# Leaving out the filler products of four linear-attention layers in an eight-block kernel on one core

## The chip, the cores and the metric

The kernel runs on one core of one Trainium2 chip. The metric is device time in microseconds (us), lower is better. Three runs of the kernel before gave 787.8, 789.82 and 791.66 us; their median is 789.82 us.

## The reference

The input is two images of 32 x 32 positions and 64 channels (2048 tokens). Six blocks follow one another, each adding to its input: a four-way selective scan with a 3x3 convolution and gates, a recurrent complex convolution in 16 steps, a softmax attention over the tokens, a two-of-eight expert layer, a stack of four linear-attention layers with eight heads each, and a spectral filter bank of 16 filters. The change lies in the fifth block. Its core, with Z of shape (2, 1024, 64):

```python
for i in range(n_layer):            # 4
    Zi = Z
    residues = jnp.zeros_like(Zi)
    for j in range(n_head):         # 8
        Attn = jnp.einsum('bni,ij,bmj->bnm', Zi, Q[i, j], Zi)
        values = jnp.einsum('ij,bnj->bni', V[i, j], Zi)
        residues = residues + jnp.einsum('bnm,bmi->bni', Attn, values) / n
    Z = Zi + residues / n_head
```

There is no softmax in it. So all of a layer can be told by the 64 x 64 matrix G = Z^T Z of each image: with S the sum over the heads of Q G V^T, the layer is Z (I + S / (n n_head)), and the next layer's G follows from this one's by two small products.

## The kernel before, in words

Every engine has its own program, written out by hand, and semaphores order them; there is no scheduler. PE works its program strictly in the order in which the code issues it.

The six blocks are stages that follow one another. In the fifth, the normed tokens are held token-major (xn); eight products of 128 x 128 add up G of both images in PSUM bank 2, and xn is turned to xn_t. Then a loop over the four layers works on 128 x 128 matrices alone, each holding the two images as diagonal blocks. Names and lines of one pass:

- L1718 (PE): T = G V for all heads, one product of 256 columns for each row pair and image. It waits for g_ready_0 (from DVE) and g_ready_1 (from ACT).
- L1053 (ACT): copies T from PSUM to t_sb.
- L1725 (PE): four products that add up S over the head pairs.
- L1343 (DVE): is_sb = I + S / (n n_head), one block for each image.
- L1731 (PE): G times is_sb, and L1348 (DVE) copies it to u_sb. L1733 (PE): the product W of all layers so far, and L1055 (ACT) copies it to wt_sb.
- L1736 (PE): the next layer's G, and L488 and L489 copy its blocks to g_two and g_sb, on DVE for the first image, on ACT for the second.

The last layer has neither L1731 nor L1736. In layer 0, ACT also scales four weight matrices (L1059) after L1055. Behind the loop L1739 turns W (ACT's L1064 copies it), L1743 applies it to all tokens, DVE adds the result (L1360), norms the tokens, and PE turns them (L1623) ahead of the filter loop (L1765, L1781).

At three places of a pass stands a call of keep_busy (line 1383; its product is line 1386): a product of the identity with the first 256 columns of the constants into PSUM bank 0, which nobody reads. It waits for nothing and signals nothing. Other such calls stand at lines 1396, 1606, 1632, 1686, 1707 and 1746, ahead of other stages.

Of the kernel before, what the change touches and what calls it, by code (L numbers as in the profile page):

```python
# [67 lines left out]
def wait(engine, sem, value):  # L68

    if isinstance(value, int) and value <= 0:  # L70
        return
    engine.wait_ge(sem, value)

def program(nc, x_cm, consts, vec, rows, w_in, conv_w, w_dt, w_bc, par, w_out, w_gate, ab, dft,
            w_qv, w_k, w_attn, w_router, w_expert, b_expert, v_t, q_t, phi, sigma, m_phi, m_u, out):
    with ExitStack() as ctx:
# [5 lines left out]
        def sig(name):  # L83
            if name not in sems:
                sems[name] = ctx.enter_context(nc.semaphore(name))
            return sems[name]
# [1291 lines left out]
        def _(pe):  # L1378
# [4 lines left out]
            def keep_busy(bank, times, cols=HALF):  # L1383

                for _ in range(times):
                    pe.matmul(ps[:, bank, 0:cols], ident, cst[:, 0:cols], start=True, stop=True)  # L1386
# [328 lines left out]
            for l in range(LAYERS):  # L1715
                for b in range(B):
                    pe.wait_ge(sig(f"g_ready_{b}"), l + 1)
                    mm = pe.matmul(ps[:, 3, b * 256:(b + 1) * 256], g_two[:, b, :], v_sb[:, l, :],  # L1718
                                   start=True, stop=True)
                mm.then_inc(sig("t_done"), 1)  # L1720
                keep_busy(0, 1, 256)
                pe.wait_ge(sig("t_out"), l + 1)
                t_pairs = t_sb.rearrange("p (b h e) -> p b h e", b=B, h=4)
                for h in range(4):
                    mm = pe.matmul(ps[:, 4, 0:P].rearrange("p (b e) -> p b e", b=B), q_sb[:, l, h, :],  # L1725
                                   t_pairs[:, :, h, :], start=(h == 0), stop=(h == 3))
                mm.then_inc(sig("s_done"), 1)
                keep_busy(0, 1, 256)
                pe.wait_ge(sig("is_ready"), l + 1)
                if l < LAYERS - 1:  # L1730
                    pe.matmul(ps[:, 5, 0:P], g_sb, is_sb, start=True, stop=True).then_inc(sig("gs_done"), 1)  # L1731
                wait(pe, sig("wt_out"), l)
                pe.matmul(ps[:, 6, 0:P], is_sb, wt_sb if l else ident, start=True, stop=True).then_inc(sig("wt_done"), 1)  # L1733
                if l < LAYERS - 1:
                    pe.wait_ge(sig("gs_out"), l + 1)
                    pe.matmul(ps[:, 7, 0:P], is_sb, u_sb, start=True, stop=True).then_inc(sig("g_done"), 1)  # L1736
                    keep_busy(0, 1, 256)
            pe.wait_ge(sig("wt_out"), LAYERS)
            pe.transpose(ps[:, 6, 0:P], wt_sb, ident).then_inc(reach("w_turned"), 1)  # L1739
            pe.wait_ge(*after("w_out_ready"))  # L1740
# [207 lines left out]
```

## Time and profile before

| what | value |
|---|---|
| median of three runs | 789.82 us |
| the profiled execution, its own time | 790.21 us |
| its span, first to last instruction | 788.4 us |
| mean granted clock of TensorE over the span | 0.977 |
| PE busy | 713.4 us (90%), 2480 instructions |
| DVE busy | 605.7 us (77%) |
| POOL busy | 413.4 us (52%) |
| ACT busy | 349.9 us (44%) |
| the four layers | 597.2 to 621.3 us of the span |
| fillers (L1386) in the whole program | 110 records, 45.0 us |

Busy time says how long an engine worked, not what waited for it; that is told by the idle time before an instruction and by its releaser, in brackets in the timeline. A product of 32-bit numbers shows as two records in the trace.

### The profile page before, as it was taken

Reading aid. Unit: us, or ns where it says so; the run is one execution under the profiler, and the core shown is the slowest. Engines: PE = TensorE matmul, PEld = TensorE weight load, DVE = VectorE, ACT = ScalarE, POOL = GpSimd, SP = SyncE. Lnnn points to the kernel's source line nnn. Section 1 sums busy time; section 2 is a strip of 40 time slices with the busy share of each in tenths; the row PEclk is TensorE's granted clock in tenths of the full one; section 3 lists DMA queues with packets and bytes.
Section 4 is the critical chain, followed back from the end, with each engine's and each line's share of the span. In section 5 each row is a group of like instructions: output and inputs, shape, how many; then the busy total and the mean of one; then the engine's idle time right before and its main releaser. Section 6 shows DMA issues by size and latency. Waiting matters only on the chain.

```text
span 788.4 us, 7109 instructions
## 1 busy us (share of the span) xinstructions
PE 713.4 (90%) x2480; PEld 358.9 (46%) x2480; DVE 605.7 (77%) x598; ACT 349.9 (44%) x387; POOL 413.4 (52%) x229
## 2 busy tenths in 40 slices
PE   6979999989899899998988868997798899999997
PEld 4633333333233233333333323465345577777775
DVE  5799999999999999999999948656793543334432
ACT  3676474556754754556544326143103243333331
POOL 3166999998999999899889900000051000000000
PEclk9979999999999999999999989999999999999999
DMA  5134564665554646536465451300730000000000
GB/s 169 62 133 140 185 212 168 220 214 175 187 180 166 236 162 207 197 137 202 157 246 176 159 214 81 106 10 1 281 145 1 1 0 1 1 1 0 0 0 27
DMA packets 30126, 97.76 MB, mean 124 GB/s; under 512 B 4132, under 2 KB 4870, under 8 KB 29358
## 3 DMA queue, kind: packets, MB, share of 16 engines
q1 hardware_dynamic: 30096, 97.38, 35.6%
q8 instruction: 16, 0.26, 0.1%
q14 instruction: 14, 0.11, 0.0%
HBM read 95.78 MB, written 1.59 MB: 123 GB/s over the span
## 4 chain that ended last, share of the span: by engine, by line
PE 42%; DVE 28%; issue 11%; POOL 9%; DMA 5%; ACT 4%; SPq 0%; DVEq 0%; POOLq 0%
PE ps L1765 15%; DVE area L1173 10%; PE ps L1460 6%; POOL area L617 6%; DVE ps L1161 5%; DMA area<-c_rows 4%; PE ps L1483 4%; PE ps L1781 4%; DVE area L1169 2%; DVE area L354 2%; PE ps L1386 2%; PE ps L1404 1%; DVE small L432 1%; POOL area L633 1%; PE ps L1451 1%
## 5 line engine op out<-in xcount | busy, mean ns | idle before, releaser
L617 POOL TENSOR_TENSOR area<-area 128x1024 f32<-128x1024 f32 x127 | 297.7, 2370 | 32.0 <-DVE area L1173 21.4
L1483 PE MATMUL ps<-area,cst 128*128 128x512 f32 x512 | 254.2, 623 | 7.1 <-POOL area L617 6.6
L1173 DVE TENSOR_TENSOR_SCAN area<-area,ps 128x1024 f32<-128x1024 f32 x111 | 249.8, 2275 | 4.1 <-ACT area L809 0.9
L809 ACT ACTIVATE area<-area,floors,par_sb 128x1024 f32<-128x1024 f32 x111 | 133.0, 1235 | 62.2 <-DVE area L1173 55.6
L1483 PEld LDWEIGHTS ps<-area,cst 128*128 128x128 f32 x512 | 89.8, 192 | 119.9 <-issue 95.5
L1161 DVE TENSOR_TENSOR ps<-ps,area 128x1024 f32<-128x1024 f32 x111 | 133.0, 1213 | 4.5 <-PE ps L1451 3.9
L1765 PE MATMUL ps<-stack,sel 128*128 128x512 f32 (+1 forms) x576 | 116.2, 362 | 0.7 <-DVE sel L1366 0.7
L1765 PEld LDWEIGHTS ps<-stack,sel 128*128 128x128 f32 x576 | 97.0, 191 | 19.7 <-issue 1.2
L464 DVE COPY area<-ps 64x1024 f32<-64x1024 f32 x32 | 39.3, 1227 | 73.6 <-PE ps L1781 41.4
L714 POOL COPY area<-area 128x256 f32 (+1 forms) x16 | 6.4, 403 | 131.3 <-PE ps L1781 131.3
L462 ACT ACTIVATE area<-ps 64x1024 f32<-64x1024 f32 x32 | 32.7, 1021 | 95.7 <-PE ps L1765 52.8
L1451 PE MATMUL ps<-stack,sel 32*128 32x512 f32 x222 | 54.1, 498 | 18.0 <-DVE area L1173 17.8
L695 POOL TENSOR_TENSOR area<-area 128x256 f32<-128x256 f32 x8 | 5.8, 728 | 120.5 <-DVE area L1319 120.5
L1451 PEld LDWEIGHTS ps<-stack,sel 32*128 32x128 f32 x222 | 20.3, 186 | 95.8 <-DVE area L1173 53.0
L1460 PE MATMUL ps<-area,cst 128*128 128x512 f32 x112 | 50.2, 600 | 6.3 <-DVE area L1173 6.3
L809 ACT ACTIVATE ps<-area,floors,par_sb 128x1024 f32<-128x1024 f32 x17 | 20.5, 1208 | 79.2 <-DVE area L1173 79.2
L1386 PE MATMUL ps<-cst 128*128 128x512 f32 (+1 forms) x110 | 45.0, 551 | 0.0
L633 POOL TENSOR_TENSOR area<-area 128x1024 f32<-128x1024 f32 x17 | 40.0, 2355 | 0.0
L1169 DVE TENSOR_TENSOR_SCAN area<-ps,area 128x1024 f32<-128x1024 f32 x17 | 38.5, 2267 | 0.0
L1460 PEld LDWEIGHTS ps<-area,cst 128*128 128x128 f32 x112 | 20.6, 190 | 34.8 <-issue 23.2
L1354 DVE TENSOR_TENSOR stack<-area,stack 128x1025 fp32r<-128x1025 f32 x16 | 19.5, 1227 | 14.8 <-ACT stack L1070 14.8
L1386 PEld LDWEIGHTS ps<-cst 128*128 128x128 f32 x110 | 21.9, 207 | 17.7 <-issue 16.5
(310 smaller groups left out, 713.2 us busy)
## 6 DMA issues: line engine op xcount, KB each, us to landing
area<-c_rows SPq DMA_DIRECT2D x145, 512.0 KB, 4.4
area<-phi_scaled SPq DMA_DIRECT2D x1, 4104.0 KB, 24.2
area<-in_m_phi_dram SPq DMA_DIRECT2D x4, 1024.0 KB, 8.2
area<-phi_scaled SPq DMA_DIRECT2D x1, 4096.0 KB, 13.8
area<-in_q_t_dram SPq DMA_DIRECT2D x1, 1024.0 KB, 13.7
c_rows<-tok SPq DMA_DIRECT2D x28, 32.0 KB, 2.8
area<-in_dft_dram SPq DMA_DIRECT2D x1, 784.0 KB
area<-in_m_u_dram SPq DMA_DIRECT2D x1, 768.0 KB, 5.8
```

What stands on the lines that cost most here:

```text
L464: engine.tensor_copy(dst, src).then_inc(sig("filtered_1"), 1)
L617: pool.tensor_tensor(scan_order(prod[:, u % PRODS, :], k), lines(state[:, u % STATES, :], k), lines(c_sb[:, u % COPIES, :], k), MUL).then_ ...
L633: pool.tensor_tensor(aid, aid, u_in[:, n % 2, :], MUL).then_inc(sig("pool_driven"), 1)
L809: act.activation(dst, delta[:, n % 2, :], ACT.Exp, bias=floors[:, k, i:i + 1], scale=par_sb[:, k, i:i + 1]).then_inc(sig("decayed"), 1)
L1161: dve.tensor_tensor(drive_pair(u), drive_pair(u), u_in[:, n % 2, :], MUL).then_inc(sig("driven"), 1)
L1169: dve.tensor_tensor_scan(state[:, u % STATES, :], banks(BANK["a", u]), aid, 0.0, MUL, ADD).then_inc(sig("scanned"), 1)
L1173: dve.tensor_tensor_scan(state[:, u % STATES, :], decay[:, u % DECAYS, :], drive_pair(u), 0.0, MUL, ADD).then_inc(sig("scanned"), 1)
L1386: pe.matmul(ps[:, bank, 0:cols], ident, cst[:, 0:cols], start=True, stop=True)
L1451: mm = pe.matmul(ps[:, BANK["b", u] + h, :], sel[at:at + 32, i, :], b_rows[at:at + 32, n % 2, :], start=True, stop=True)
L1460: mm = pe.matmul(ps[:, BANK["soft", n] + h, :], ident, half(term, h), start=(at == 0), stop=(at == 3))
L1483: mm = pe.matmul(ps[:, 6 + h, :], con("center"), half(prod[:, u % PRODS, :], h), start=(u % (UNITS // 2) == 0), stop=(u % (UNITS // 2) == ...
L1765: mm = pe.matmul(ps[:, 2 + 2 * (g % 2) + y, :].rearrange("p (a n) -> p a n", a=2)[:, :, P * (at - 2 * y):2 * P], xn_hl[:, x_part, j * P:(j ...
```

## The change

The three calls of keep_busy inside the layer loop are taken out. Nothing else differs; the other six calls stay.

```diff
@@ -1718,14 +1718,12 @@
                     mm = pe.matmul(ps[:, 3, b * 256:(b + 1) * 256], g_two[:, b, :], v_sb[:, l, :],
                                    start=True, stop=True)
                 mm.then_inc(sig("t_done"), 1)
-                keep_busy(0, 1, 256)
                 pe.wait_ge(sig("t_out"), l + 1)
                 t_pairs = t_sb.rearrange("p (b h e) -> p b h e", b=B, h=4)
                 for h in range(4):
                     mm = pe.matmul(ps[:, 4, 0:P].rearrange("p (b e) -> p b e", b=B), q_sb[:, l, h, :],
                                    t_pairs[:, :, h, :], start=(h == 0), stop=(h == 3))
                 mm.then_inc(sig("s_done"), 1)
-                keep_busy(0, 1, 256)
                 pe.wait_ge(sig("is_ready"), l + 1)
                 if l < LAYERS - 1:
                     pe.matmul(ps[:, 5, 0:P], g_sb, is_sb, start=True, stop=True).then_inc(sig("gs_done"), 1)
@@ -1734,7 +1732,6 @@
                 if l < LAYERS - 1:
                     pe.wait_ge(sig("gs_out"), l + 1)
                     pe.matmul(ps[:, 7, 0:P], is_sb, u_sb, start=True, stop=True).then_inc(sig("g_done"), 1)
-                    keep_busy(0, 1, 256)
             pe.wait_ge(sig("wt_out"), LAYERS)
             pe.transpose(ps[:, 6, 0:P], wt_sb, ident).then_inc(reach("w_turned"), 1)
             pe.wait_ge(*after("w_out_ready"))
```

PE's program of one layer (l=1) before, to the first product of the next; L1386 is the filler, the other names are those of the list above:

```order
L1718 MATMUL ps<-area 128x256 x2
L1386 MATMUL ps<-cst 128x256
L1725 MATMUL ps<-area 128x128 x4
L1386 MATMUL ps<-cst 128x256
L1731 MATMUL ps<-area 128x128
L1733 MATMUL ps<-area 128x128
L1736 MATMUL ps<-area 128x128
L1386 MATMUL ps<-cst 128x256
L1718 MATMUL ps<-area 128x256 x2
```

The same in the changed program, where L1725 has become line 1724, L1731 1729, L1733 1731 and L1736 1734:

```order
L1718 MATMUL ps<-area 128x256 x2
L1724 MATMUL ps<-area 128x128 x4
L1729 MATMUL ps<-area 128x128
L1731 MATMUL ps<-area 128x128
L1734 MATMUL ps<-area 128x128
L1718 MATMUL ps<-area 128x256 x2
```

Three products are gone, and no other has changed its place. In the last layer, with what follows it, PE's program before:

```order
L1718 MATMUL ps<-area 128x256 x2
L1386 MATMUL ps<-cst 128x256
L1725 MATMUL ps<-area 128x128 x4
L1386 MATMUL ps<-cst 128x256
L1733 MATMUL ps<-area 128x128
L1739 MATMUL ps<-cst,area 128x128
L1743 MATMUL ps<-area 128x128 x8
L1386 MATMUL ps<-cst 128x512 x7
```

And in the changed program:

```order
L1718 MATMUL ps<-area 128x256 x2
L1724 MATMUL ps<-area 128x128 x4
L1731 MATMUL ps<-area 128x128
L1736 MATMUL ps<-cst,area 128x128
L1740 MATMUL ps<-area 128x128 x8
L1386 MATMUL ps<-cst 128x512 x7
```

Here two are gone, and the seven fillers behind L1743 stay. In all PE's program is shorter by 11 products; the programs of DVE, ACT and SP are the same, and so is POOL's but for line numbers.

## Rows read from the trace of the kernel before

**Rows 1.** Timeline, one layer (l=2): start, duration, engine, line, xcount [idle before <-releaser].

```profile
610.56 1.13 PE L1718 MATMUL ps<-area 128*128 128x256 f32 x4 [0.33 <-DVE area L489]
...
611.53 0.59 PE L1386 MATMUL ps<-cst 128*128 128x256 f32 x2
611.73 0.60 ACT L1053 ACTIVATE area<-ps 128x512 f32<-128x512 f32 x1 [1.33 <-PE ps L1718]
...
612.38 1.16 PE L1725 MATMUL ps<-area 128*128 128x128 f32 x8 [0.26 <-ACT area L1053]
...
613.38 0.60 PE L1386 MATMUL ps<-cst 128*128 128x256 f32 x2
613.58 0.46 DVE L1343 SCALAR_TENSOR_TENSOR area<-ps,cst 64x64 f32<-64x64 f32 x2 [3.07 <-PE ps L1725]
...
614.09 0.49 PE L1731 MATMUL ps<-area 128*128 128x128 f32 x2
...
614.96 0.49 PE L1736 MATMUL ps<-area 128*128 128x128 f32 x2 [0.16 <-DVE area L1348]
...
615.28 0.60 PE L1386 MATMUL ps<-cst 128*128 128x256 f32 x2
...
615.95 0.22 DVE L489 COPY area<-ps 64x64 f32<-64x64 f32 x1
...
616.22 1.13 PE L1718 MATMUL ps<-area 128*128 128x256 f32 x4 [0.34 <-DVE area L489]
```

**Rows 2.** Groups of PE, 597.2 to 621.3: xcount | busy us, mean ns | idle before.

```profile
L1386 PE MATMUL ps<-cst 128*128 128x256 f32 x22 | 6.6, 380 | 0.0
```

**Rows 3.** Stretch of the layers: length, busy of PE, PEld, DVE, ACT, POOL, then PEclk.

```profile
597.20:621.30 24.10, 18.88 (x93) 12.40 (x92) 4.61 (x20) 8.78 (x28) 3.49 (x4) 1.00 0.00 1
```

**Rows 4.** Timeline between layers 0 and 1, PE and ACT.

```profile
602.53 0.49 PE L1736 MATMUL ps<-area 128*128 128x128 f32 x2 [0.16 <-DVE area L1348]
602.58 2.12 ACT L1059 ACTIVATE area<-area,small 128x384 f32<-128x384 f32 x4
...
603.78 0.70 PE L1718 MATMUL ps<-area 128*128 128x256 f32 x2 [0.34 <-DVE area L489]
...
605.34 0.70 PE L1718 MATMUL ps<-area 128*128 128x256 f32 x2 [0.86 <-ACT area L489]
```

**Rows 5.** Other stretches with their granted clock, columns as in rows 3.

```profile
42.80:53.00 10.20, 8.96 (x16) 3.77 (x17) 9.26 (x8) 6.92 (x6) 5.96 (x4) 0.50 0.45 154
...
292.40:294.40 2.00, 2.00 (x8) 0.70 (x6) 2.00 (x2) 1.13 (x2) 2.00 (x2) 1.00 0.62 203
629.40:633.30 3.90, 1.71 (x10) 1.24 (x11) 3.27 (x5) 2.45 (x5) 0.00 (x0) 1.00 0.00 0
633.30:636.70 3.40, 3.40 (x11) 2.72 (x10) 0.00 (x0) 0.00 (x0) 0.00 (x0) 0.50 0.00 0
537.70:541.10 3.40, 1.43 (x11) 1.20 (x12) 3.14 (x5) 1.02 (x1) 0.00 (x0) 1.00 0.00 0
541.10:544.50 3.40, 3.02 (x13) 1.98 (x13) 0.28 (x1) 1.02 (x1) 0.00 (x0) 0.51 0.00 0
```

**Rows 6.** Timeline of PE: four records of 512 columns at two places.

```profile
48.28 3.78 PE L1483 MATMUL ps<-area,cst 128*128 128x512 f32 x4
...
292.47 1.98 PE L1483 MATMUL ps<-area,cst 128*128 128x512 f32 x4
```

**Rows 7.** Timeline behind the layers, PE and DVE.

```profile
621.30 2.05 PE L1743 MATMUL ps<-area 128*128 128x128 f32 x16 [0.37 <-ACT area L1064]
...
622.23 2.36 DVE L1354 TENSOR_TENSOR stack<-area,stack 128x1025 fp32r<-128x1025 f32 x2 [2.54 <-ACT stack L1070]
...
623.19 6.17 PE L1386 MATMUL ps<-cst 128*128 128x512 f32 x14
...
630.86 1.26 PE L1623 MATMUL ps<-cst,area 128*128 128x128 f32 x8 [1.50 <-DVE area L444]
```

## The prediction

> **What bounds the kernel now.** I read the stretch that the diff touches first, instruction by instruction, then the same stretch by group, then the granted clock around it and in other places. Rows 1 are one whole layer (l=2): the reader is to follow who releases whom. L1718 (PE) is waited for by L1053 (ACT), that by L1725 (PE), that by L1343 (DVE), that by L1731 (PE), then a copy on DVE (L1348, not shown), L1736 (PE), L489 (DVE), and the next layer's L1718 at 616.22, so 5.66 us a layer [rows 1]. No engine is full here; the layer is one round trip after another between PE, ACT and DVE, and it is as long as its latencies and its four groups of real products. The fillers (L1386) stand in the pauses. The stretch of the four layers, 597.2 to 621.3, ran at a granted clock of 1.00, the upper of the two levels (2.4 GHz), all the way [rows 3].
>
> **The change, part by part.**
>
> Removed: 11 products of 256 columns, not 12, for the last layer has no third place. They are 22 records of 380 ns, 6.6 us busy [rows 2], with no idle time before them; the trace shows every product as two records. None is waited for. What they hide matters only if the real product behind one of them starts late. Each of the three places in the layer, from rows 1:
> - After L1718: the filler ends at 611.53+0.59 = 612.12. L1053 ends at 611.73+0.60 = 612.33, and L1725 starts at 612.38. The filler is done 0.21 us before the release.
> - After L1725: it ends at 613.98; L1343 ends at 614.04 and L1731 starts at 614.09. Done 0.06 us before.
> - After L1736: it ends at 615.88; L489 ends at 616.17 and L1718 starts at 616.22. Done 0.29 us before.
> In all three the real product starts 0.05 us after its releaser's end. So no filler is on the path, and taking away 6.6 us of PE work takes 0 off the span directly: its cover was the waits for ACT and DVE. There is no added instruction, wait or transfer, no DMA, and DVE, ACT, POOL and SP keep their programs.
>
> What goes with the fillers is PE's continuity. Between the real products of layer 2, PE then idles 612.38-611.69 = 0.69, 614.09-613.54 = 0.55, 0.16 before L1736 and 616.22-615.45 = 0.77: 2.17 of 5.66 us, where it idles 0.26+0.11+0.16+0.34 = 0.87 now [rows 1]. Between layers 0 and 1 it is sparser, since ACT is held for 2.12 us by L1059: from 603.02, the end of layer 0's L1736, to 606.73, where layer 1's L1725 starts (the L1718 at 605.34 ends at 606.04, and 0.69 follows as in layer 2), only two groups of 0.70 us remain, so 2.31 of 3.71 us idle [rows 1, 4].
>
> Now the clock. Just before the filter loop PE ran 1.71 us in 3.90 (2.19 idle) and the granted clock was 0.50 for the 3.4 us behind it; at 537.7 it ran 1.43 us in 3.40 (1.97 idle) and the clock was 0.51 behind that [rows 5]. The lull between layers 0 and 1 without fillers (2.31 idle of 3.71) is as sparse as those two, and the layers after it idle 2.17 of 5.66. I therefore expect the clock to fall to the lower level (1.2 GHz) by layer 1. It came back behind 541.1, after PE had been busy 3.02 of 3.40 us at the low level; it stayed low from 42.8 to 53.0 although PE was busy 8.96 of 10.20 us [rows 5]. A layer without fillers at the low level idles the same 2.17 us of about 7.9, more than a quarter: nearer to the stretch in which it stayed low than to that after which it came back.
>
> The price of the low level. Four products' records of 512 columns (L1483) took 1.98 us at 292.47 under a clock of 1.00 and 3.78 us at 48.28 inside the stretch at 0.50: 0.45 us more for each, so about 0.225 for 256 columns and 0.11 for 128 [rows 5, 6]. A layer has on its path 4 records of 256 columns (L1718, 0.90), 8 of 128 (L1725, 0.90) and 2+2 of 128 (L1731 and L1736, 0.45): 2.25 us. L1733's two run beside DVE's copy. Bounds for the stage:
> - Lower: the clock stays at 1.00, 0 us.
> - Upper: low from layer 0's L1725 on. Layer 0: 0.90+0.45, and 0.45 for the one pair of L1718 behind the ACT wait, 1.80. Layers 1 and 2: 2.25 each. Layer 3: L1725 0.90, L1733 0.23, L1739 0.11, so 1.24. Sum 7.54. Behind it L1743's 16 records would need 1.8 more, with 624.59-623.35 = 1.24 us to spare behind DVE's L1354, so 0.6; the 14 records of the next filler end at 629.36 and have 1.50 us before L1623, and one low stretch of 3.4 us delays them by 1.7, so 0.2 [rows 7]. In all 8.3 us.
> The value I take: low from layer 1 on, 2.25+2.25+1.24 = 5.74, less one return to the upper level for 3.4 us, the length of the shorter low stretches. In 3.4 us a low layer loses 3.4 x 2.25/7.9 = 0.97, so 4.8 us. It is nearer to the upper end since the lull that I expect to bring the clock down comes early and nothing dense follows before L1743.
>
> The Trainium skill bears on this place twice, in the page "TensorE: Matmul & The Clock Gate". Its section "Why this matters for your kernels" warns of long pauses between bursts of matmuls, longer than any pause left here; by that rule the clock would stay up and the sum be 0. The trace does not agree: before the low stretch at 633.3 the longest pause was the 1.50 us ahead of L1623 [rows 7]. Its section "A second HAM failure mode: psum-queue depth-cycling" says that short, frequent idling between groups lets the clock swing between its levels; by that one the sum would lie between the bounds, near 2.9 us.
>
> The loop's first products, in turn, ran 3.40 us at the low level from 633.3 on, with PE busy throughout [rows 5]: 1.7 us that the version before lost there in this execution. I leave that in both versions.
>
> Sum: 790.21 us is the profiled execution's own time (its span 788.4 and 1.8 around it); plus 4.8 is 795.0. It lies 0.4 above the median of the three runs, 789.82, so 794.6 as a median.
>
> **The rivals.**
> 1. The clock swings: it falls in the lull, comes back after a low stretch, falls again. Over some 20 us that makes three low stretches of 3.4 us, 3 x 0.97 = 2.9 us, 792.7. For it: at 541.1 it came back after one such stretch. Against it: PE worked with hardly a pause there, and would not here.
> 2. No change: the clock stays at the upper level for all four layers. Then the layer's round trips are what they are, and the time is 789.8. For it: the three groups and their pauses repeat evenly, no single pause passes 0.9 us, and the longest pause before the fall at 633.3 was 1.50 us. Against it: the lull of layer 0 to 1. It decides if the first whole pass of layers 0 and 1 shows 1.00.
> 3. Faster: the upper level is kept in the layers, and in the same run the low stretch at the loop's start (1.7 us) goes: 789.8-1.7 = 788.1. Nothing in the program between L1743 and the loop changes, so only the moment of the fall could move. This is not over 0.5%.
> 4. The change doesn't do what it says: fillers left in place. The program shows 11 rows fewer on PE and the same rows elsewhere, so I give it no chance.
>
> **How the numbers follow.** Low from about layer 1 on: 0.58, 794.6, with its own range from 793.6 (a return of twice that length, 5.74-1.94 = 3.8) to 798.1 (the upper bound, 789.8+8.3). Swinging: 0.24, around 792.7. No change: 0.15, around 789.8. Faster: 0.03, 788.1. What can be told from no change is 0.5%, 3.9 us, so slower begins at 793.8. The first case lies over it in nine of ten, the swinging one in one of ten: 0.55. Faster by over 0.5% would need 785.9, below what any mechanism here gives; I keep 0.03 for one that I don't see. The rest, 0.42, is within 0.5%. The range goes from 790.2, which leaves out most of the no-change case, to 798.2.
>
> **What would show it.** In the profile after: no L1386 between 597 and 621; DVE's, ACT's and PE's latencies in a layer at the upper level unchanged, with real products 0.05 us after their releasers; a granted clock clearly under 1.00 over the four layers, with L1725's group of 8 near 2.0 us in place of 1.16; a layer near 7.9 us in place of 5.66; the stage longer by about 4.8 us, and all before it and the loop's rounds behind its start as they were. I am wrong if the clock reads 1.00 there (rival 2), if low and high stretches alternate (rival 1), or if a layer at the upper level is shorter than 5.66 us, which would mean that a filler held the real products back.

## The result, and the profile after

The changed kernel took 796.92 us (median of four runs, 796.05 to 798.97); the kernel before took 790.32 us in the four runs beside it. The ratio is 1.0091, with a 95% interval of 1.0057 to 1.0125: slower by 0.9%. Run once more beside the kernel before, it gave 797.97 against 789.91 us, ratio 1.0088 (1.0063 to 1.0112).

The stretch of the four layers is where it happens. In the changed program L1725 has become L1724, L1731 L1729, L1733 L1731, L1736 L1734, L1739 L1736, L1743 L1740 and L1765 L1762. The timeline of the changed kernel (start, duration, engine, line, count of records, idle time before and its releaser):

```profile
607.62 0.70 PE L1718 MATMUL ps<-area 128*128 128x256 f32 x2 [0.77 <-DVE area L489]
...
609.17 0.70 PE L1718 MATMUL ps<-area 128*128 128x256 f32 x2 [0.85 <-ACT area L489]
...
610.55 2.07 PE L1724 MATMUL ps<-area 128*128 128x128 f32 x8 [0.69 <-ACT area L1053]
...
615.92 2.07 PE L1718 MATMUL ps<-area 128*128 128x256 f32 x4 [0.77 <-DVE area L489]
618.03 0.60 ACT L1053 ACTIVATE area<-ps 128x512 f32<-128x512 f32 x1 [2.28 <-PE ps L1718]
...
618.68 2.07 PE L1724 MATMUL ps<-area 128*128 128x128 f32 x8 [0.69 <-ACT area L1053]
...
620.79 0.46 DVE L1343 SCALAR_TENSOR_TENSOR area<-ps,cst 64x64 f32<-64x64 f32 x2 [4.93 <-PE ps L1724]
...
621.30 0.80 PE L1729 MATMUL ps<-area 128*128 128x128 f32 x2 [0.55 <-DVE area L1343]
...
622.48 0.80 PE L1734 MATMUL ps<-area 128*128 128x128 f32 x2
...
624.05 2.07 PE L1718 MATMUL ps<-area 128*128 128x256 f32 x4 [0.77 <-DVE area L489]
...
626.81 2.07 PE L1724 MATMUL ps<-area 128*128 128x128 f32 x8 [0.69 <-ACT area L1053]
...
630.59 0.47 PE L1736 MATMUL ps<-cst,area 128*128 128x128 f32 x1 [0.37 <-ACT area L1055]
...
634.92 1.22 DVE L1360 TENSOR_TENSOR tok<-tok,ps 128x1024 f32<-128x1024 f32 x1 [0.20 <-PE ps L1740]
...
641.16 1.26 PE L1623 MATMUL ps<-cst,area 128*128 128x128 f32 x8 [0.27 <-DVE area L444]
```

Beside [rows 1]: ACT's and DVE's instructions last as long as before (0.60, 0.46), and a real product starts 0.05 us after its releaser as before. What changed is PE's groups: L1718's four records take 2.07 in place of 1.13 us, L1724's eight 2.07 in place of 1.16, L1729's and L1734's two 0.80 in place of 0.49. That is 0.94+0.91+0.31+0.31 = 2.47 us a layer, and the layer from 615.92 to 624.05 is 8.13 us in place of 5.66. The group of eight at 610.55 is the first long one; the two of L1718 just ahead of it are still 0.70.

The granted clock says the same. The stretches of the changed kernel (length, busy time of PE, PEld, DVE, ACT and POOL, then the clock):

```profile
601.10:609.50 8.40, 4.76 (x22) 2.98 (x22) 1.38 (x6) 4.65 (x14) 2.13 (x3) 1.00 0.01 2
...
610.70:630.60 19.90, 14.97 (x47) 10.91 (x47) 3.21 (x14) 3.13 (x11) 0.30 (x1) 0.50 0.00 0
630.60:634.30 3.70, 3.33 (x14) 3.04 (x15) 1.94 (x2) 2.17 (x3) 0.00 (x0) 0.50 0.00 0
...
643.20:650.00 6.80, 6.80 (x34) 5.73 (x35) 2.24 (x2) 2.31 (x3) 0.00 (x0) 1.00 0.01 2
```

Where [rows 3] has 1.00 all the way, the clock is 1.00 up to the end of the lull between layers 0 and 1 and then 0.50 for the rest of the stage and on through L1740, from 610.7 to 634.3, 23.6 us on end. The filter loop, which began at 0.50 before [rows 5], began at 1.00.

The two traced executions differ by 8.8 us in span (788.4 and 797.2). Of that, 6.15 is the stage from the first L1718 to the product behind the layers (601.13 to 630.59, before 597.29 to 620.60), 0.31 the way from there to the loop (12.56 and 12.25), and -1.50 the loop and what follows. The other 3.84 lies ahead of the stage, where both programs are the same: over the traced executions of all kernels that share that part, the first L1718 came between 596.63 and 601.50 us. So the part that the change itself can be seen to make is 6.15+0.31 = 6.46 us. Whether the change also took off the loop's 1.50 us is taken up below; other traces speak against it.

### The profile page after: what moved, and what is told of

Same layout as the page of the kernel before. It is cut to its first block, busy times and chain, and to the rows that moved or that the text cites. A ratio compares the mean times of both kernels' runs of the same rounds, so it can differ in the third digit from the quotient of the medians.

```text
span 797.2 us, 7065 instructions
## 1 busy us (share of the span) xinstructions
PE 719.3 (90%) x2458; PEld 362.9 (46%) x2458; DVE 603.6 (76%) x598; ACT 349.7 (44%) x387; POOL 413.6 (52%) x229
## 4 chain that ended last, share of the span: by engine, by line
PE 49%; DVE 28%; issue 10%; POOL 5%; ACT 4%; DMA 4%; DVEq 0%; SPq 0%; POOLq 0%
PE ps L1762 14%; DVE area L1173 10%; PE ps L1483 8%; PE ps L1460 6%; DVE ps L1161 5%; PE ps L1778 4%; DMA area<-c_rows 3%; POOL area L617 2%; DVE area L1169 2%; PE ps L1451 2%; DVE area L354 2%; PE ps L1386 2%; PE ps L1404 1%; DVE small L432 1%; PE ps L1724 1%
## 5 line engine op out<-in xcount | busy, mean ns | idle before, releaser
L1762 PE MATMUL ps<-stack,sel 128*128 128x512 f32 (+1 forms) x576 | 114.7, 359 | 0.7 <-DVE sel L1366 0.7
L1762 PEld LDWEIGHTS ps<-stack,sel 128*128 128x128 f32 x576 | 95.9, 189 | 19.3 <-issue 1.2
L1386 PE MATMUL ps<-cst 128*128 128x512 f32 (+1 forms) x88 | 38.7, 598 | 0.0
L1778 PE MATMUL ps<-area 128*64 128x128 f32 (+2 forms) x256 | 29.4, 382 | 0.0
```

What stands on the lines that cost most here:

```text
L1762: mm = pe.matmul(ps[:, 2 + 2 * (g % 2) + y, :].rearrange("p (a n) -> p a n", a=2)[:, :, P * (at - 2 * y):2 * P], xn_hl[:, x_part, j * P:(j ...
L1778: mm = pe.matmul(ps[64 * b:64 * b + 64, lo // 256, :].rearrange("p (t n) -> p t n", t=2)[:, :, lo % 256:lo % 256 + hi - lo], w_work[:, a, ...
```

## Experiments

Each experiment was traced in one execution; the medians are over all its runs. The theory under test: the fillers do nothing for the layers but hold the granted clock at its upper level; without them the clock falls, and the layers' real products, which are on the path, take twice the stream time. The rival: a real product costs a fixed 0.59 us more (6.46/11) when no filler stands ahead of it, whatever the clock. "Stage" is the time from the first L1718 to the product behind the layers: 23.31 us before, 29.46 in the changed kernel.

**Fillers in layers 0 and 1 only** (e1; at all three places):

```diff
-                keep_busy(0, 1, 256)
+                if l < 2:
+                    keep_busy(0, 1, 256)
```

> Fillers in layers 0 and 1 only (6 of the 11 products). Theory (the fillers' only work is to hold the granted clock): clock 1.00 through layers 0 and 1, at 5.66 us a layer; it may fall in layer 2 or 3, and each low layer is then about 8.1 us as in the changed kernel. L1718 of layer 0 to the last L1725 group's end of the stage: 0 to 3.5 us longer than before. Rival (each filler left out costs a fixed start-up time, 6.46/11 = 0.59 us, whatever the clock): layers 0 and 1 as before, 2 and 3 longer by 5 x 0.59 = 2.9 us at a clock of 1.00.

Measured: 790.39 against 789.67 us, ratio 1.0014 (0.9997 to 1.003); ten runs from 789.15 to 794.77. The traced one, at 794.7 one of the two longest, by stretches:

```profile
600.90:614.20 13.30, 10.10 (x49) 6.43 (x49) 2.77 (x12) 6.07 (x19) 3.49 (x4) 1.00 0.00 1
614.20:620.00 5.80, 3.64 (x19) 2.62 (x20) 1.38 (x6) 1.42 (x5) 0.00 (x0) 1.00 0.00 0
620.40:626.30 5.90, 4.30 (x14) 2.80 (x12) 0.44 (x2) 0.87 (x2) 0.00 (x0) 0.50 0.00 0
```

Layer 2, without a filler, ran at 1.00 and took 619.84-614.18 = 5.66 us: three products without a filler ahead, no cost. Layer 3 was low. The stage took 25.05 us, 1.74 longer, within the theory's 0 to 3.5 and against the rival's clock of 1.00.

**Fillers in layers 2 and 3 only** (e2; at all three places):

```diff
-                keep_busy(0, 1, 256)
+                if l >= 2:
+                    keep_busy(0, 1, 256)
```

> Fillers in layers 2 and 3 only (5 of the 11). Theory: the clock falls in the lull between layers 0 and 1 or in layer 1, and layers 2 and 3 with fillers leave PE hardly a pause, so the clock comes back after one short low stretch: 2 to 4 us longer than before. Should it stay low all the same, the fillers at the low level (0.86 us each where the pauses are 0.55 to 0.77) delay the real products and the stage is as long as without fillers, 6.5 us or more over before. Rival (fixed cost for each filler left out): 6 x 0.59 = 3.5 us longer, with the clock at 1.00.

Measured: 791.66 against 789.67 us, ratio 1.0038 (1.0011 to 1.0065); six of ten runs lie from 791.21 to 791.69 and four from 794.93 to 798.36. In the traced execution, one of those four:

```profile
599.66 0.70 PE L1718 MATMUL ps<-area 128*128 128x256 f32 x2 [0.60 <-ACT area L489]
...
601.05 1.81 PE L1726 MATMUL ps<-area 128*128 128x128 f32 x8 [0.69 <-ACT area L1053]
```

```profile
601.50:614.80 13.30, 9.82 (x31) 6.70 (x29) 2.75 (x12) 4.27 (x13) 3.48 (x4) 0.50 0.00 0
614.90:618.40 3.50, 3.50 (x9) 2.59 (x10) 0.00 (x0) 0.60 (x1) 0.00 (x0) 0.50 0.00 0
618.60:626.30 7.70, 6.35 (x35) 4.27 (x33) 1.83 (x8) 1.70 (x6) 0.00 (x0) 1.00 0.00 1
```

Here the clock fell in layer 0 already: its L1718 still takes 0.70 us, the group behind it (L1725, now line 1726) 1.81 in place of 1.16. Up to there this program is that of the changed kernel, so the place of the fall is not fixed. The clock came back in layer 2 as soon as the fillers left PE no pause (3.50 of 3.50 us). The stage took 27.8 us. The fall was earlier than expected and the low stretch longer than one short one; without fillers in layers 2 and 3 (the changed kernel) the clock did not come back there.

**Only the third filler of a layer** (e3):

```diff
                 mm.then_inc(sig("t_done"), 1)
-                keep_busy(0, 1, 256)
...
                 mm.then_inc(sig("s_done"), 1)
-                keep_busy(0, 1, 256)
```

> Only the third filler of a layer, behind L1736 (3 of the 11). PE then idles about 1.6 us of each layer of 5.66 and the lull between layers 0 and 1 has one filler. Theory: whatever happens goes with the clock; if it falls the layers behind are near 8 us and the stage 4 to 7 us longer, if it holds 0. Rival (fixed cost for each filler left out): 8 x 0.59 = 4.7 us longer with the clock at 1.00.

and **only the first** (e4):

```diff
                 mm.then_inc(sig("s_done"), 1)
-                keep_busy(0, 1, 256)
...
                     pe.matmul(ps[:, 7, 0:P], is_sb, u_sb, start=True, stop=True).then_inc(sig("g_done"), 1)
-                    keep_busy(0, 1, 256)
```

> Only the first filler of a layer, behind L1718 (4 of the 11). PE idles about 1.6 us of each layer. Theory: as for the third place alone: 0 if the clock holds, 4 to 7 us if it falls, no dependence on the place as such. Rival (fixed cost for each filler left out): 7 x 0.59 = 4.1 us longer with the clock at 1.00.

Measured: e3 790.79 us, ratio 1.002 (0.9994 to 1.0046), ten runs from 788.23 to 798.57; e4 791.16 us, ratio 1.0029 (1.0002 to 1.0057), ten runs from 788.32 to 798.97. The two traced executions happened to fall on either side, and they decide between the theories. Of e3, stretch, two starts of L1718 and the group behind the second:

```profile
601.80:625.40 23.60, 20.09 (x58) 13.30 (x56) 4.16 (x18) 5.92 (x19) 3.48 (x4) 0.50 0.00 0
```

```profile
614.93 2.08 PE L1718 MATMUL ps<-area 128*128 128x256 f32 x4
...
623.07 2.08 PE L1718 MATMUL ps<-area 128*128 128x256 f32 x4
...
625.83 1.16 PE L1724 MATMUL ps<-area 128*128 128x128 f32 x8 [0.69 <-ACT area L1053]
```

Of e4, the same, and from its loop's start the L1623 ahead of it and the first stretch:

```profile
601.50:624.80 23.30, 15.49 (x77) 10.68 (x77) 4.59 (x20) 8.34 (x26) 3.49 (x4) 1.00 0.00 1
...
637.10:640.50 3.40, 3.40 (x17) 2.87 (x18) 0.00 (x0) 0.34 (x1) 0.00 (x0) 1.00 0.02 5
```

```profile
605.86 0.49 PE L1730 MATMUL ps<-area 128*128 128x128 f32 x2 [0.55 <-DVE area L1343]
...
614.76 1.13 PE L1718 MATMUL ps<-area 128*128 128x256 f32 x4 [0.77 <-DVE area L489]
...
620.41 1.13 PE L1718 MATMUL ps<-area 128*128 128x256 f32 x4 [0.77 <-DVE area L489]
...
635.05 1.26 PE L1623 MATMUL ps<-cst,area 128*128 128x128 f32 x8 [1.50 <-DVE area L444]
```

In e4 seven of the 11 products are gone, the pauses of 0.55 and 0.77 stand open, the clock held, and the layer is 620.41-614.76 = 5.65 us; the stage is 23.29, that of before. In e3 the clock fell, in layer 0, and the layer is 8.14 us; the clock came back behind the last L1718 (the group at 625.83 takes 1.16 us again), read 1.00 up to 628.3 and was low again from 628.9 to 632.1. The stage took 29.82 us. A layer is as long as its clock says, not as its fillers say. The rival is out. The spread of the ten runs of each kernel fits a clock that falls in some executions with one filler a layer and not in others; more than one of each was not traced.

**All fillers at half the size** (e5; at all three places):

```diff
-                keep_busy(0, 1, 256)
+                keep_busy(0, 1, 128)
```

> All 11 fillers in place, each with 128 columns in place of 256, so 0.22 us of work each. PE then idles about 1.5 us of each layer. Theory: the time is decided by whether the clock holds: in the traced execution either 1.00 throughout and 5.66 us a layer, or a low stretch with layers near 8.1 us; the median 0 to 3 us over before. Rival (a fixed start-up cost where no filler stands ahead): no product lacks a filler ahead of it, so 0 whatever the clock.

Measured: 790.04 against 789.68 us, ratio 1.0 (0.998 to 1.0019). Even so the clock fell once in the traced execution, in the lull, and came back:

```profile
605.27 0.64 PE L1386 MATMUL ps<-cst 128*128 128x128 f32 x2
606.16 2.08 PE L1725 MATMUL ps<-area 128*128 128x128 f32 x8 [0.26 <-ACT area L1053]
```

```profile
605.30:608.50 3.20, 2.94 (x13) 2.51 (x11) 0.22 (x1) 0.60 (x1) 1.09 (x2) 0.50 0.00 0
608.70:621.00 12.30, 8.86 (x51) 6.94 (x51) 2.80 (x13) 3.13 (x11) 0.00 (x0) 1.00 0.00 1
```

That cost 24.28-23.31 = 0.97 us of stage, the price for one short low stretch. It is also the reverse of e4: here L1725 had its filler ahead and took 2.08 us all the same, where the rival had 0.

**All fillers, but the stage entered low** (e6):

```diff
-            keep_busy(3, 8)
             for j in range(TILES):
```

> All 11 fillers in place, but the eight products of 512 columns ahead of the stage (line 1707) are left out, so PE idles some 6 us before the layers and enters them at the low level. Theory: L1711's 16 records take about 3.5 us in place of 2.05 and the first layer or two run near 8 us, until the clock returns, as it did in layer 2 of the kernel with fillers in layers 2 and 3 only; 2 to 5 us over before, with the very instructions of before in the layers. Rival (what counts is the filler ahead of each product, not the clock): layers at 5.66 us, 0 to 1 us over before.

Measured: 792.52 against 789.68 us, ratio 1.0036 (1.0014 to 1.0059). In the traced execution (L1711 is L1710 there, L1718 L1717):

```profile
590.80:600.80 10.00, 5.08 (x24) 5.08 (x25) 6.49 (x30) 0.92 (x3) 0.00 (x0) 0.50 0.00 0
601.00:624.50 23.50, 18.48 (x93) 12.20 (x91) 4.59 (x20) 8.31 (x25) 3.48 (x4) 1.00 0.00 1
```

The first layers were not slow, against the expectation: L1711's and L1623's 24 records ahead of them ran one behind the other at the low level, and the clock was back by 601. The loss was there: from L1711's start to L1718's it took 600.97-595.72 = 5.25 us in place of 597.29-594.31 = 2.98, so 2.27 of the 2.8 us. For the layers this run decides nothing between the theories; it says that the entry alone does not keep them low.

**Two fillers in the lull alone** (e7: behind L1718 of layer 1, behind L1736 of layer 0, and none behind L1725):

```diff
-                keep_busy(0, 1, 256)
+                if l == 1:
+                    keep_busy(0, 1, 256)
...
-                keep_busy(0, 1, 256)
...
-                    keep_busy(0, 1, 256)
+                    if l == 0:
+                        keep_busy(0, 1, 256)
```

> Two fillers alone, in the lull between layers 0 and 1: behind L1736 of layer 0 and behind L1718 of layer 1. If the lull is what brings the clock down, as the prediction had it, the clock holds through the stage and the time is within 1.5 us of before. If the layers' own pauses of 0.55 to 0.77 us are enough, it falls one layer later or so and the stage is 3 to 6 us longer. Rival (fixed cost for each filler left out): 9 x 0.59 = 5.3 us longer at a clock of 1.00.

Measured: 792.17 against 789.68 us, ratio 1.0039 (1.0014 to 1.0064); no run of ten was under 791.14.

```profile
596.60:609.80 13.20, 8.35 (x40) 5.37 (x40) 2.73 (x12) 6.08 (x19) 3.48 (x4) 1.00 0.00 1
...
612.10:623.40 11.30, 8.38 (x28) 6.05 (x27) 1.83 (x8) 1.70 (x6) 0.00 (x0) 0.50 0.00 1
```

The clock passed the lull at 1.00 and fell in layer 2. So the lull is not needed: the layers' own pauses, none over 0.77 us, are enough. In e2 the clock had fallen before it came to the lull. The stage took 26.75 us.

**The changed kernel again** (e9, the diff of the change):

> The changed kernel itself once more, beside the kernel before on the same chip. Theory (without fillers the layers' pauses bring the clock down in every execution, and nothing in the stage brings it back): no execution as short as the median of before; the traced one has a fall in layers 0 to 2, low layers of 8.1 us up to L1736, and a stage (first L1718 to L1736) of 26 to 30 us in place of 23.3; median 4 to 7 us over before. If the clock's fall is a matter of chance in each execution, as it was with one filler a layer, some executions are within 1 us of before.

Six runs from 794.24 to 799.95, none as short as the median of before. The traced one fell at the same point and stayed low to the stage's end; its stage is 29.46 us again:

```profile
601.00:610.30 9.30, 5.12 (x22) 2.94 (x22) 1.38 (x6) 5.15 (x15) 2.92 (x4) 1.00 0.01 2
610.50:630.50 20.00, 15.09 (x47) 11.02 (x47) 3.21 (x14) 3.13 (x11) 0.36 (x1) 0.50 0.00 0
```

**More fillers** (e8): what held the clock in the layers might hold it elsewhere.

```diff
+            keep_busy(7, 8, 256)
             pair_mean(2)
+            keep_busy(5, 4, 256)
             pe.wait_ge(sig("gn_out"), 2)
...
             for h in range(2):
+                keep_busy(7, 1 + 2 * h, 256)
                 pe.wait_ge(sig("q_ready"), h + 1)
...
-            keep_busy(6, 7)
+            keep_busy(6, 8)
             turn(tile(xn), 0, 10)
+            keep_busy(6, 1, 256)
```

> The kernel before with fillers added at three stretches where the clock is low or falls: 8 and 4 products of 256 columns about the second group norm (463 to 468 us), 1 and 3 in the waits for L1668 (537 to 541), one more of 512 columns ahead of the last L1623 and one of 256 behind it (630 to 633). Theory: the low stretches at 466, 541 and 633 go; L1579's first 8 records take 1.9 us in place of 3.68, L1668 to L1676 lose about 1.4 us, the loop's start up to 1.7: 2 to 5 us faster than before. If the added products delay real ones or the clock falls elsewhere, 0 to 2 us slower.

Measured: 784.56 against 789.68 us, ratio 0.9927 (0.9909 to 0.9945): faster than the kernel before. The places in the kernel before, and in e8 (L1581 is L1579, L1671 L1668, L1679 L1676):

```profile
467.85 3.68 PE L1579 MATMUL ps<-area,cst 128*64 128x512 f32 x8 [2.11 <-DVE area L1223]
...
540.76 1.66 PE L1668 MATMUL ps<-cst,area 128*128 128x128 f32 x8 [1.68 <-DVE area L1269]
...
543.12 2.63 PE L1676 MATMUL ps<-area 128*64 128x512 f32 x8 [0.38 <-DVE area L1274]
```

```profile
466.69 1.94 PE L1581 MATMUL ps<-area,cst 128*64 128x512 f32 x8 [0.28 <-DVE area L1223]
...
537.64 1.09 PE L1671 MATMUL ps<-cst,area 128*128 128x128 f32 x8 [0.39 <-DVE area L1269]
...
539.28 1.94 PE L1679 MATMUL ps<-area 128*64 128x512 f32 x8 [0.38 <-DVE area L1274]
```

L1579's eight gain 1.74 us; from the second L1668 to L1676's end it was 545.75-540.76 = 4.99 us and is 541.22-537.64 = 3.58, so 1.41; from the loop's first product to the end of the span it was 788.4-632.85 = 155.55 and is 782.4-628.33 = 154.07, so 1.48. Together that is 4.63, beside the 5.1 by the medians. The third part is that of this pair of traces; that it stands in the medians is not shown, as the next run says.

**The loop's start alone** (e10):

```diff
-            keep_busy(6, 7)
+            keep_busy(6, 8)
             turn(tile(xn), 0, 10)
+            keep_busy(6, 1, 256)
```

> The kernel before with one more product of 512 columns ahead of the last L1623 and one of 256 behind it, nothing else. Theory (the pauses of 1.50 and 0.73 us there bring the clock down at the loop's start in some executions, at 1.7 us each): 0 to 1.7 us faster in the median, no low stretch at the loop's start in the traced execution. If the loop's start does not matter: 0.

Measured: 788.84 against 789.91 us, ratio 0.9989 (0.9972 to 1.0005). The loop's start ran at 1.00 in the traced execution (from 631.6 to 638.0), but the gain in the median can't be told from none, and other executions without these two fillers ran it at 1.00 too (below).

**The added fillers, and none in the layers** (e11: the diff of e8 and that of the change together):

> The added fillers of the three other stretches, but none in the four layers: the change made to the faster kernel. Theory: the loss of the layers stands by itself, so 4 to 7 us over the 784.6 us of the kernel with the added fillers, 789 to 792 us, with low layers of 8.1 us. If the low stretches ahead of the layers had a part in the loss, less than 4 us over it.

Measured: 794.08 against 789.91 us, ratio 1.0062 (1.0037 to 1.0086), and 9.5 over e8: more than expected. The layers lost as they did in the changed kernel (stage 29.48, in e8 23.29; clock 0.50 from 602.9 to 629.9). Some of the rest is a filler that has become a delay:

```profile
627.85 8.13 PE L1386 MATMUL ps<-cst 128*128 128x512 f32 x16
...
635.82 1.04 PE L1625 MATMUL ps<-cst,area 128*128 128x128 f32 x8
```

The 16 records ahead of the transposes, 7.03 us in e8, began at the low level, took 8.13 and held them to 635.82, 1.5 us behind their input; from the product behind the layers to the loop it is 13.51 us against 12.25. These two parts make 7.45 us. The two traced spans differ by 8.6 (791.0 and 782.4), and the other 1.16 lies ahead of the stage, where the two programs are the same (first L1718 at 593.95 and 592.79). The rest of the 9.5 was not settled; e8 and e11 were not timed side by side.

## Why the prediction was right, point by point

- **Nothing of the fillers on the path.** Right. With the clock held, a layer with no filler (e1's layer 2) or with one of three (e4) is 5.66 or 5.65 us.
- **The clock falls by layer 1.** Right in place: the second L1718 of the lull [rows 4] still takes 0.70 us, and the group behind it, layer 1's L1724, is the first at the low level. It fell there in all three traced executions without a filler in the layers (the changed kernel twice, and e11). The reason given, the lull, was too narrow: e7 filled it and the clock fell in layer 2, and in e2 it fell in layer 0, in the very program of the changed kernel up to there, behind pauses of 0.60 and 0.69 us. The Trainium skill's page "TensorE: Matmul & The Clock Gate", section "Why this matters for your kernels", warns of long pauses; by that rule the clock should have held. The trace does not agree: in the changed kernel's stage no pause ahead of the fall was over 0.85 us.
- **It stays low, less one return.** Half right, and the term that was mis-sized most. The sum took off 0.97 us for a return to the upper level for 3.4 us; there was none in the stage in either traced execution of the changed kernel, nor in e11. That it would mostly stay low was right, but in part by luck: the two rows that the prediction set against each other, busy 3.02 of 3.40 us where the clock came back and 8.96 of 10.20 where it stayed low [rows 5], show nearly the same share, so they could not tell which to expect. A return did come in e5, where smaller fillers were left, and later ones in e2 and e3. The Trainium skill tells, in the page "TensorE: Matmul & The Clock Gate", section "A second HAM failure mode: psum-queue depth-cycling", of a clock that swings between its levels. The traces of e5 and e3 show one that fell, came back and in e3 fell again; those of the changed kernel show one fall and no return in the stage.
- **The price of a low layer.** 2.25 us forecast, 2.47 measured. The two large groups came as worked out (0.94 and 0.91 against 0.90 each); the pairs of L1729 and L1734 cost 0.31 each and not 0.225. The sum priced them by the record, from a group of long records; what the other 0.09 us of a pair is was not tested. Counted as in the prediction, from L1724 to L1724, layers 1 and 2 lost 2.48 and 2.47 and the rest 1.22: 6.17, where 5.74 stood before the return was taken off.
- **Behind the stage.** L1740 ran low and DVE's L1360 waited 0.20 us for it, 0.31 in all, inside the bound of 0.6. The next fillers ended before L1623's input, so their 0.2 did not come.
- **The loop's start.** Taken as the same in both; in this pair of executions it was not, -1.50 us. L1740 took 3.45 us in place of 2.05, so the seven fillers behind it ended later, while DVE's chain to L1623 lost 0.31 us only, and PE's pause ahead of L1623 shrank from 1.50 [rows 7] to 0.27 us. But that pause does not settle at which level the loop begins: in e4 it stood in full, and the loop began at 1.00 (the last lines of e4's rows). From the loop's first product to the end of the span e4, e5 and e6, all three with the pause of 1.50, took 154.0 to 154.1 us, and the changed kernel 154.05; of all the traces only those of the kernel before (155.55) and of e2 (155.53) had the low start. So the 1.50 us can't be put down to the change.
- **The sum.** 4.8 forecast; 6.46 by the traces, 6.6 by the medians (8.1 in the second comparison). What lies between 4.8 and 6.46 is, to within 0.1, the return that did not come (0.97), the layers' price (6.17 in place of 5.74) and the 0.31 behind the stage. The time, 796.92, lies inside the range of 790.2 to 798.2, 2.3 over the value; of the ten single runs of the changed kernel, four lie above the range, up to 799.95.

## What to carry to other kernels

A product that computes nothing can carry the speed of all real products near it: judge it by the granted clock in the stretch and by the length of the real groups behind it, not by its own place off the path. Where an engine's short groups are links of a round trip, price both levels of the clock from rows of the same shape, and take the state in which it would stay, not a mean. And look for the other low stretches: filling three more waits with such products gave 0.7% here. A filler is free only while it ends before the next real product's release; at the low level the same filler is longer (in e3 1.06 us in place of 0.60) and may not.

## What the runs showed that was not expected

- Fillers of half the size did as well as full ones in the median (790.04 against 789.68 us), and one a layer did nearly as well (790.79 and 791.16); but single runs of these went up to 794.77, 798.57 and 798.97 us. A median of few runs can so hide a filler that is too small.
- The level at which a stretch runs is not told by how busy PE is in it: e4's layers, PE busy 15.49 of 23.30 us, kept the upper level, while e3's, 20.09 of 23.60, and the changed kernel's, 14.97 of 19.90, stayed at the lower for all of those stretches. At the lower level the same products also take longer, so the busy shares of two levels don't compare.
- A group of two records of 128 columns takes 0.49 us at the upper level and 0.80 at the lower, less than twice; eight take 1.16 and 2.07.
